# First layer's cross attention: another order of TensorE's work inside a step

## The chip, the cores and the metric

The kernel runs on one core of a Trainium2 chip. It is one launch that computes a whole two-layer decoder. The metric is the device time of that launch in microseconds (us), as the median of several runs. TensorE is called PE below, VectorE DVE, ScalarE ACT, GpSimd POOL and SyncE SP.

## The reference, cut to what matters

The first layer does self attention, cross attention, and a mixture of experts; the second layer follows. Only the cross attention matters here:

```
x = _layernorm(x + _L0_attn_ref(...))
x = _layernorm(x + _L0_xattn_ref(x, ctx_2048, ctx_2048, L0_xattn_gamma))   # this one
...
# inside _L0_xattn_ref: q, k, v are [32, 64, 256]; 8 heads cut the 64 rows in eights,
# the attention runs over the 256 columns
qk = jnp.einsum('bhdq,bhdl->bhql', qh, kh) * scale
sm = jax.nn.softmax(qk, axis=-1)
ret = jnp.einsum('bhql,bhdl->bhdq', sm, vh)
```

So there are 32 x 8 = 256 heads, each with a 256 x 256 matrix of scores over a depth of only 8.

## The kernel before, in words

The 2048 rows of x are 16 tiles of 128 rows; a tile holds two batch entries, so 16 heads. `cross_attention` works in **steps**; a step is two heads, and eight steps (`STEPS`) are a tile. Tile s owns steps 8s to 8s+7, and n is the step's number in its tile. Three things happen to a head, in different steps:

- **First pass** (`first_pass`, PE, L964). The scores of two heads with 3 x 8 x 3 = 72 rows of contraction (q and k are split into bf16 parts), four matmuls of 256 columns into one of two PSUM buffers `a_s` and `a_pt` (even and odd steps). DVE reduces the whole buffer to the negated maxima of 512 rows (`maxima`, L866, output `b_nm`). The first pass of a step waits for the maxima of the step two earlier, since they share a buffer.
- **Second pass** (`second_pass`, PE, L995), 14 steps later (`LAG`). The same scores with three more rows that hold the maxima, two matmuls for each head, into `a_qkv` (even head) or `a_y` (odd head). ACT takes the exponentials (`exps`, L918) into `a_late`. The second pass of a head waits for the exponentials of the head two earlier.
- **Values** (`values`, PE, L1010), from 17 steps on. Four heads are multiplied by their values in one call, into `a_o`: for each of two halves of the keys (`lh`), four matmuls with 32 output columns each, side by side in the array. They are f32, and each matmul is two instructions, so a call shows as sixteen. It runs in every second step. When two calls have filled both halves of `a_o`, ACT copies them out (`products_out`, L924), and the next call waits for that copy.

Small work hangs on single steps. After the last step of a tile DVE splits the maxima in three bf16 parts (`split_maxima`, L879 to L887); PE turns them at n = 2 (`turn_maxima`, L982), ACT copies them (`maxima_out`, L930), SP sends them into the operands of the second pass. At n = 4 DVE takes reciprocals of the denominators of the tile three back (`inverse`, L891), at n = 6 the statistics of its norm (L897, L899). At n = 4 PE turns the normed tile of four back (`turn`, L1020) and ACT copies it (L934).

Each engine runs its own instructions in the order in which they are written, and semaphores link them. The order inside a step on PE was:

```
first_pass(step) ; turn_maxima ; second_pass(both heads) ; values(four heads, every second step) ; turn
```

The first six first passes (`AHEAD`) stand in the self attention before. Steps 6 to 13 have a first pass alone, 14 to 127 have first and second pass, 128 to 141 a second pass alone. When all 16 tiles are normed, the mixture of experts starts.

Of the kernel before, what the change touches and what calls it, by code (L numbers as in the profile page):

```python
# [25 lines left out]
P = 128  # L26
B, T, D = 32, 64, 256
NTOK = B * T
TILES = NTOK // P
SEQS = P // T  # L30
KD = D // P
# [30 lines left out]
class Kernel:  # L62
# [23 lines left out]
    def sem(self, name):  # L86
        self.sems.append(self.nc.alloc_semaphore(name=name))
        return self.sems[-1]
# [579 lines left out]
def cross_attention(k, ctx, free):  # L668
# [3 lines left out]

    nc, io, sem = k.nc, k.io, k.sem
    G, DT, L = P // 8, 8, D
    ROWS = 9 * DT
    SCALE = float(DT) ** -0.5
    STEPS = G // 2
    LAG = STEPS + 6  # L680
    HEADS_2 = G // 2
    qparts = nc.dram_tensor("qparts", (TILES, 3, DT, G, L), BF16, kind="Internal").ap()
    def sb(name, shape, dt=F32):
        return k.sb("b_" + name, shape, dt, ctx)

    def many(count, name, shape, dt=F32):
        return [sb(f"{name}{v}", shape, dt) for v in range(count)]
# [4 lines left out]
    ks, qs = ([space.take([G, L], BF16) for space in (front, middle)] + [sb(n, [P, G, L], BF16)] for n in ("ks", "qs"))  # L692
    vt = many(2, "vt", [P, KD, G, 32])
    nm, nrest, mp = many(2, "nm", [P, 2 * G]), many(2, "nrest", [P, 2 * G]), many(2, "mp", [P, 3, 2 * G], BF16)
    mt = many(2, "mt", [96, P], BF16)
    pr, os_, nd = late.many(8, [KD, L]), end.many(2, [4, L]), end.many(3, [4, L])
# [3 lines left out]
    s2 = [bank[:].rearrange("p (a n) -> p a n", n=L) for bank in (qkv_bank, y_bank)]  # L700
    o_ps = o_bank[:].rearrange("p (a b) n -> p a (b n)", a=2)
# [3 lines left out]
    split, vt_done = sem("b_split"), sem("b_vt_done")  # L705
# [5 lines left out]
    s2_full, s2_out, pv_done, o_out = sem("b_s2_full"), sem("b_s2_out"), sem("b_pv_done"), sem("b_o_out")  # L711
# [7 lines left out]
    T_AT, REC_AT, STATS_AT, TURN_AT = 2, 4, 6, 4  # L719
# [6 lines left out]
    def live(t):  # L726
        return 0 <= t < TILES
# [185 lines left out]
    def scalar(act):  # L913
        def exps(x, g):
            act.wait_ge(s2_full, G * x + g + 1)
            if g % 4 == 0 and 4 * x + g // 4 >= 2:
                act.wait_ge(pv_done, 4 * x + g // 4 - 1)
            act.activation(pr[g % 8][:], s2[g % 2][:], ACT.Exp, scale=SCALE).then_inc(s2_out, 1)  # L918

        def products_out(t, half):  # L920
            act.wait_ge(pv_done, 4 * t + 2 * half + 2)
            if t >= 2:
                act.wait_ge(nd_in[(t - 2) % 3], 64 * ((t - 2) // 3 + 1))
            act.activation(os_[t % 2][:, 2 * half:2 * half + 2, :], o_ps[:], ACT.Copy).then_inc(o_out, 1)  # L924

        def maxima_out(t):
            act.wait_ge(mp_turned, t + 1)
            if t >= 2:
                act.wait_ge(m_placed[t % 2], 16 * (t // 2))
            act.activation(mt[t % 2][:], trb[0:96, :], ACT.Copy).then_inc(mt_out, 1)  # L930

        def turned_out(t):
            act.wait_ge(rn_turned, t + 1)
            act.activation(k.residT[:, :, t * P:(t + 1) * P], tr[:, 0:KD, :], ACT.Copy).then_inc(rT_out, 1)  # L934

        for step in range(LAST):
            s, n = divmod(step, STEPS)
            if n == T_AT and live(s - 1):
                maxima_out(s - 1)
            x, j = divmod(step - LAG, STEPS)  # L940
            if live(x):
                exps(x, 2 * j)
            y, at = divmod(step - LAG - 4, STEPS)
            for half in range(2):
                if at == 4 * half + 2 and live(y):
                    products_out(y, half)
            if live(x):
                exps(x, 2 * j + 1)
            if n == TURN_AT and live(s - 4):
                turned_out(s - 4)  # L950

    def first_pass(pe, step):
        s, n = divmod(step, STEPS)
        if n % 4 == 0:
            pe.wait_ge(placed[s % 3][n // 4], 64 * (s // 3 + 1) + (16 if n == 0 else 0))
        if step == 0:
            pe.wait_ge(free.shifted, TILES)
        elif step == 1:
            pe.wait_ge(free.pt_out, TILES)
        else:  # L960
            pe.wait_ge(s1_out, step - 1)
        for g in (2 * n, 2 * n + 1):
            for qh in range(2):
                ins = pe.matmul(s1[step % 2][:, g % 2, qh, :], qs[s % 3][0:ROWS, g, qh * P:(qh + 1) * P],  # L964
                                ks[s % 3][0:ROWS, g, :], start=True, stop=True)
        ins.then_inc(s1_full, 1)
# [5 lines left out]
    def tensor(pe):  # L972
        def turn_maxima(t):
            if t == 0:
                pe.wait_ge(free.qT_out, TILES)
                pe.wait_ge(free.kbd_out, 4 * TILES)
            pe.wait_ge(m_split, t + 1)
            if live(t - 4):
                pe.wait_ge(rT_out, t - 3)
            if t >= 1:  # L980
                pe.wait_ge(mt_out, t)
            pe.transpose(trb[0:96, :], mp[t % 2][:].rearrange("p a n -> p (a n)"), k.identb[:]).then_inc(mp_turned, 1)  # L982

        def second_pass(x, j):
            if x == 0 and j == 0:
                pe.wait_ge(free.qk_out, TILES)
                pe.wait_ge(free.v_out, 2 * TILES)
                pe.wait_ge(free.y_out, TILES)
            if j == 0:
                pe.wait_ge(m_placed[x % 2], 16 * (x // 2 + 1))  # L990
            for g in (2 * j, 2 * j + 1):
                if G * x + g >= 2:
                    pe.wait_ge(s2_out, G * x + g - 1)
                for lh in range(KD):
                    ins = pe.matmul(s2[g % 2][:, lh, :], ks[x % 3][0:ROWS + 3, g, lh * P:(lh + 1) * P],  # L995
                                    qs[x % 3][0:ROWS + 3, g, :], start=True, stop=True)
                ins.then_inc(s2_full, 1)

        def values(x, q):
            pe.wait_ge(s2_out, G * x + 4 * q + 4)  # L1000
            if x == 0 and q == 0:
                pe.wait_ge(free.o_out, TILES)
            if q == 0:
                pe.wait_ge(vt_done, 2 * x + 2)
            if q % 2 == 0 and 2 * x + q // 2 > 0:
                pe.wait_ge(o_out, 2 * x + q // 2)
            for lh in range(KD):
                for j in range(4):
                    g = 4 * q + j
                    ins = pe.matmul(o_ps[32 * j:32 * j + 32, q % 2, :], vt[x % 2][:, lh, g, :], pr[g % 8][:, lh, :],  # L1010
                                    start=(lh == 0), stop=(lh == KD - 1))
            ins.then_inc(pv_done, 1)

        def turn(t):
            pe.wait_ge(rn_done, t + 1)
            pe.wait_ge(mt_out, min(t + 4, TILES))
            if t >= 1:
                pe.wait_ge(rT_out, t)
            for kd in range(KD):
                ins = pe.transpose(tr[:, kd, :], nd[t % 3][:, 3, kd * P:(kd + 1) * P], k.ident[:])  # L1020
            ins.then_inc(rn_turned, 1)

        for step in range(LAST):
            s, n = divmod(step, STEPS)
            if live(s) and step >= AHEAD:
                first_pass(pe, step)
            if n == T_AT and live(s - 1):
                turn_maxima(s - 1)
            x, j = divmod(step - LAG, STEPS)
            if live(x):  # L1030
                second_pass(x, j)
            y, at = divmod(step - LAG - 3, STEPS)
            if live(y) and at % 2 == 0:
                values(y, at // 2)
            if n == TURN_AT and live(s - 4):
                turn(s - 4)

    return (Programs(sync, gpsimd, scalar, vector, tensor),
            Programs(sync_between, gpsimd_between, None, vector_between, tensor_between))

# [7 lines left out]
def layer0_cross_attention(k):  # L1048
# [3 lines left out]
    with k.memory as ctx:  # L1052
        second, between = cross_attention(k, ctx, free)
        with k.nc.Block() as block:
            @block.sync
            def _(sp):
                first.sync(sp, between.sync)
                second.sync(sp)

            @block.gpsimd  # L1060
            def _(gp):
                first.gpsimd(gp, between.gpsimd)
                second.gpsimd(gp)

            @block.scalar
            def _(act):
                first.scalar(act)
                second.scalar(act)

            @block.vector  # L1070
            def _(dve):
                first.vector(dve, between.vector)
                second.vector(dve)

            @block.tensor
            def _(pe):
                first.tensor(pe, between.tensor)
                second.tensor(pe)
# [2099 lines left out]
```

## Time and profile before

| | before |
|---|---|
| median of 3 runs | 1250.38 us (1249.96 to 1255.8) |
| the profiled execution's own time | 1244.66 us |
| its span | 1242.6 us |
| PE, DVE, ACT, POOL busy | 1103.5, 800.7, 585.0, 454.7 us |
| mean granted PE clock | 0.969 of full |

The span goes from the first to the last instruction of the profiled execution. A busy PE in this table is not a PE at its peak, since the ends of matmuls are modelled and neighbours overlap; what the engine can do is read from the distance between starts. The cross attention fills the span from about 163 us (its first first pass) to about 427 us (its last transpose).

### The profile page before, as it was taken

The page shows a single profiled execution, that of the slowest core. Times are in us where ns is not written, and L with a number is a line of the kernel's source. Part 1 is how long each engine was busy: PE and PEld are TensorE (multiplying, and loading weights), DVE is VectorE, ACT ScalarE, POOL GpSimd, SP SyncE. Part 2 cuts the span into 40 slices and gives each one's busy share as a digit, 9 for nine tenths or more (in the row PEclk, how much of TensorE's full clock was granted, in tenths as well). Part 3 has the DMA queues.
Part 4 walks back from the last instruction along what each step waited for, and adds up shares of the span by engine and source line. Part 5 has one row for each costly group of instructions (what it writes and reads, how often), then busy time and mean ns, then how long its engine had stood idle before and what let it go on. Part 6 is the DMA issues. An engine that isn't in the chain of part 4 may idle for free. (4 is left out here: it accounts for less than half of the span.)

```text
span 1242.6 us, 20732 instructions
## 1 busy us (share of the span) xinstructions
PE 1103.5 (89%) x7356; PEld 652.4 (53%) x7356; DVE 800.7 (64%) x1547; ACT 585.0 (47%) x1209; POOL 454.7 (37%) x692
## 2 busy tenths in 40 slices
PE   6888769998998599999878999869997999999997
PEld 3566535454554245777433555647775343545455
DVE  4899886888886142333576668647885456465555
ACT  2666506766767331343376555348773422121110
POOL 6999851555534245333235346431111000000001
PEclk9999978999999799999999999989997999999999
DMA  6964354655662112453503000020000000000000
GB/s 219 309 192 143 94 131 106 147 139 142 149 143 73 47 56 97 125 170 120 174 1 135 1 1 1 1 69 2 2 2 5 21 1 0 9 9 9 8 9 26
DMA packets 75354, 95.90 MB, mean 77 GB/s; under 512 B 12883, under 2 KB 62189, under 8 KB 74573
## 3 DMA queue, kind: packets, MB, share of 16 engines
q1 hardware_dynamic: 70835, 84.92, 24.1%
q0 software_dynamic: 3408, 9.34, 2.1%
q8 instruction: 61, 1.00, 0.3%
q10 hardware_dynamic: 1010, 0.31, 0.1%
q14 instruction: 40, 0.33, 0.1%
HBM read 57.47 MB, written 31.27 MB: 71 GB/s over the span
## 5 line engine op out<-in xcount | busy, mean ns | idle before, releaser
L918 ACT ACTIVATE a_late<-a_qkv 128x512 f32<-128x512 f32 x128 | 77.3, 604 | 59.3 <-PE a_qkv L995 59.3
L2654 POOL TENSOR_SCALAR f_rstd<-f_mv 128x1 f32<-128x1 f32 x16 | 3.8, 239 | 266.5 <-DVE f_mv L2793 266.4
L866 DVE TENSOR_REDUCE b_nm<-a_s 128x4 f32<-128x1024 f32 x64 | 78.0, 1219 | 30.8 <-PE a_s L964 30.8
L2738 DVE TENSOR_TENSOR f_prod<-f_sg,f_kept 128x512 f32<-128x512 f32 (+1 forms) x48 | 33.2, 692 | 96.4 <-ACT f_kept L2683 93.5
L2863 PE MATMUL fps_h<-residT,w_f_w 128*128 128x512 f32 x176 | 82.4, 608 | 2.5 <-DVE f_inner L2775 2.5
L866 DVE TENSOR_REDUCE b_nm<-a_pt 128x4 f32<-128x1024 f32 x64 | 76.7, 1199 | 2.3 <-PE a_pt L964 2.3
L918 ACT ACTIVATE a_late<-a_y 128x512 f32<-128x512 f32 x128 | 77.0, 602 | 0.0
L2677 ACT ACTIVATE f_sg<-fps_h 128x512 f32<-128x512 f32 (+1 forms) x24 | 14.3, 596 | 125.2 <-PE fps_h L2882 108.3
L1010 PE MATMUL a_o<-a_late,b_vt 128*32 128x256 f32 x1024 | 69.2, 389 | 0.0
L1320 POOL DMA_INDIRECT routed<-c_out,c_target x39 | 37.4, 959 | 67.2 <-ACT c_out L1401 66.9
L1974 DVE SCALAR_TENSOR_TENSOR d_acc<-d_pad,d_cw,d_acc 128x512 f32<-128x512 f32 x72 | 58.4, 815 | 4.9 <-ACT d_acc L1880 3.2
L350 POOL TENSOR_TENSOR a_nrm<-a_ss,phalf 128x20 f32<-128x20 f32 x16 | 56.9, 3559 | 3.5 <-DVE a_ss L472 3.5
L2863 PEld LDWEIGHTS fps_h<-residT,w_f_w 128*128 128x128 f32 x176 | 33.3, 193 | 42.1 <-issue 37.7
L1520 DVE TENSOR_TENSOR c_hid<-c_sg,cps_h 128x176 f32<-128x176 f32 x39 | 13.2, 338 | 63.1 <-ACT c_sg L1395 63.1
L1582 PE MATMUL cps_h<-c_wgu,c_xT 128*128 x156 | 52.7, 461 | 0.6 <-ACT c_xT L1389 0.6
L2100 PE MATMUL cps_h<-residT,d_win 128*128 128x512 f32 x96 | 46.6, 617 | 3.4 <-ACT d_zs L1873 1.9
L838 POOL TENSOR_TENSOR a_rest<-a_rest 128x256 f32<-128x256 f32 x16 | 11.6, 723 | 96.1 <-DVE a_rest L891 96.1
L1805 POOL TENSOR_TENSOR d_rs<-d_ms,mhalf 128x4 f32<-128x4 f32 x16 | 22.4, 1400 | 65.7 <-DVE d_ms L2031 65.7
L1314 POOL DMA_INDIRECT xrows<-c_xr,c_place_int x32 | 31.0, 967 | 35.0 <-DVE c_xr L1490 19.8
L2677 ACT ACTIVATE f_sg<-f_kept 128x512 f32<-128x512 f32 (+1 forms) x24 | 15.1, 630 | 60.1 <-DVE f_kept L2743 60.1
L1010 PEld LDWEIGHTS a_o<-a_late,b_vt 128*32 128x32 f32 x1024 | 26.9, 110 | 25.1 <-issue 14.0
L1601 PE MATMUL cps_o<-c_wd,c_hT 88*128 x156 | 40.1, 380 | 0.0
(428 smaller groups left out, 2896.9 us busy)
## 6 DMA issues: line engine op xcount, KB each, us to landing
kparts<-a_rest SPq DMA_DIRECT2D x48, 192.0 KB, 3.8
a_rest<-a_rest SPq DMA_DIRECT2D x64, 128.0 KB, 3.0
xrows<-in_c_fill SPq DMA_DIRECT2D x13, 387.0 KB, 4.5
c_xrow<-xrows SPq DMA_DIRECT2D x39, 129.0 KB, 2.1
c_back<-routed SPq DMA_DIRECT2D x16, 256.0 KB, 3.6
a_front<-kparts SPq DMA_DIRECT2D x12, 288.0 KB
a_front<-qparts SPq DMA_DIRECT2D x36, 96.0 KB
qparts<-b_xp SPq DMA_DIRECT2D x48, 64.0 KB, 2.8
```

Source lines behind the costliest of these rows:

```text
L350: gp.tensor_tensor(nrm[v][:], ss[v][:], k.phalf[:, 0:H20], ALU.pow).then_inc(rooted, 1)
L866: dve.tensor_reduce(nm[s % 2][:, 4 * n:4 * n + 4].rearrange("p (g h) -> p g h", h=2), s1[step % 2][:], AX.X, ALU.max, negate=True).then_in ...
L918: act.activation(pr[g % 8][:], s2[g % 2][:], ACT.Exp, scale=SCALE).then_inc(s2_out, 1)
L1010: ins = pe.matmul(o_ps[32 * j:32 * j + 32, q % 2, :], vt[x % 2][:, lh, g, :], pr[g % 8][:, lh, :], start=(lh == 0), stop=(lh == KD - 1))
L1314: gp.indirect_dma_start(k.xrows[:], bass.IndirectOffsetOnAxis(ap=place_int[n][:, t:t + 1], axis=0), xr[:, t, :], None).then_inc(scattered[ ...
L1320: gp.indirect_dma_start(routed[:], bass.IndirectOffsetOnAxis(ap=target[s % 8][:], axis=0), out[s % 4][:], None).then_inc(sent[s % 4], 16)
L1582: ins = pe.matmul(h_ps[s % 2][:, 0:2 * F], xT[s % 2][:, kd, :], wgu[:, kd, ds(e, 1), :].rearrange("p a f -> p (a f)"), start=(kd == 0), st ...
L1601: ins = pe.matmul(o_ps[:, s % 2, 0:D], hT[s % 2][:, c, :], wd2[:, ds(e, 1), c, :].rearrange("p a f -> p (a f)"), start=(c == 0), stop=(c = ...
L1974: ins = dve.scalar_tensor_tensor(out=acc[v][:], in0=pad[v][:, :, tap:tap + T], scalar=cw[:, m, tap:tap + 1], in1=acc[v][:], op0=ALU.mult, ...
L2100: ins = pe.matmul(bank[:], win[:, kd, m * P:(m + 1) * P] if m < XT else wz[:, kd, (m - XT) * P:(m - XT + 1) * P], k.residT[:, kd, c * CHUN ...
L2738: dve.tensor_tensor(prod[n % 2][at], sg[n % 2][at], up, ALU.mult).then_inc(prod_done, 1)
L2863: pe.matmul(h_ps[j][:], (w1, w3)[j][:, kd, m * P:(m + 1) * P], k.residT[:, kd, c * CHUNK:(c + 1) * CHUNK], start=(kd == 0), stop=False)
```

## The change

The PE step is written in another order, and the calls are cut smaller. `second_pass` now takes one head, `values` one half of the keys of four heads. A step is now: half a `values` call, the second pass of the even head, the first pass, `turn_maxima`, the second pass of the odd head, `turn`. ACT's step follows it: `products_out` first, then the even head's exponentials, `maxima_out`, the odd head's exponentials. A blank line moves the numbers of the lines behind it by one.

```
@@ scalar (ACT) @@
-            if n == T_AT and live(s - 1):
-                maxima_out(s - 1)
-            x, j = divmod(step - LAG, STEPS)
-            if live(x):
-                exps(x, 2 * j)
             y, at = divmod(step - LAG - 4, STEPS)
             for half in range(2):
                 if at == 4 * half + 2 and live(y):
                     products_out(y, half)
+            x, j = divmod(step - LAG, STEPS)
+            if live(x):
+                exps(x, 2 * j)
+            if n == T_AT and live(s - 1):
+                maxima_out(s - 1)
             if live(x):
                 exps(x, 2 * j + 1)
@@ tensor (PE) @@
+        def values(x, q, lh):
+            if lh == 0:
+                pe.wait_ge(s2_out, G * x + 4 * q + 4)
+                if x == 0 and q == 0:
+                    pe.wait_ge(free.o_out, TILES)
+                if q == 0:
+                    pe.wait_ge(vt_done, 2 * x + 2)
+                if q % 2 == 0 and 2 * x + q // 2 > 0:
+                    pe.wait_ge(o_out, 2 * x + q // 2)
+            for j in range(4):
+                g = 4 * q + j
+                ins = pe.matmul(o_ps[32 * j:32 * j + 32, q % 2, :], vt[x % 2][:, lh, g, :], pr[g % 8][:, lh, :],
+                                start=(lh == 0), stop=(lh == KD - 1))
+            if lh == KD - 1:
+                ins.then_inc(pv_done, 1)
...
         for step in range(LAST):
             s, n = divmod(step, STEPS)
+            y, at = divmod(step - LAG - 3, STEPS)
+            if live(y):
+                values(y, at // KD, at % KD)
+            x, j = divmod(step - LAG, STEPS)
+            if live(x):
+                second_pass(x, 2 * j)
             if live(s) and step >= AHEAD:
                 first_pass(pe, step)
             if n == T_AT and live(s - 1):
                 turn_maxima(s - 1)
-            x, j = divmod(step - LAG, STEPS)
             if live(x):
-                second_pass(x, j)
-            y, at = divmod(step - LAG - 3, STEPS)
-            if live(y) and at % 2 == 0:
-                values(y, at // 2)
+                second_pass(x, 2 * j + 1)
             if n == TURN_AT and live(s - 4):
                 turn(s - 4)
```

**Two steps on PE where everything runs** (steps 22 and 23; `b_ks,b_qs` are the operands of the first pass, `a_middle` those of the second). Before:

```order
L964 MATMUL a_s<-b_ks,b_qs 128x256 x4
L995 MATMUL a_qkv<-a_middle 128x256 x2
L995 MATMUL a_y<-a_middle 128x256 x2
L964 MATMUL a_pt<-b_ks,b_qs 128x256 x4
L995 MATMUL a_qkv<-a_middle 128x256 x2
L995 MATMUL a_y<-a_middle 128x256 x2
L1010 MATMUL a_o<-a_late,b_vt 32x256 x8
```

Now, from the half call that opens step 22:

```order
L1010 MATMUL a_o<-a_late,b_vt 32x256 x4
L995 MATMUL a_qkv<-a_middle 128x256 x2
L965 MATMUL a_s<-b_ks,b_qs 128x256 x4
L995 MATMUL a_y<-a_middle 128x256 x2
L1010 MATMUL a_o<-a_late,b_vt 32x256 x4
L995 MATMUL a_qkv<-a_middle 128x256 x2
L965 MATMUL a_pt<-b_ks,b_qs 128x256 x4
L995 MATMUL a_y<-a_middle 128x256 x2
```

The count of matmuls is the same. The block of eight that stood between two odd-to-even pairs is now two blocks of four, one ahead of each even head, and the first pass stands between the two heads.

**Where the second pass sets in, on PE** (steps 14 and 15). Before:

```order
L964 MATMUL a_s<-a_middle 128x256 x4
L995 MATMUL a_qkv<-a_front 128x256 x2
L995 MATMUL a_y<-a_front 128x256 x2
L964 MATMUL a_pt<-a_middle 128x256 x4
L995 MATMUL a_qkv<-a_front 128x256 x2
L995 MATMUL a_y<-a_front 128x256 x2
```

Now:

```order
L995 MATMUL a_qkv<-a_front 128x256 x2
L965 MATMUL a_s<-a_middle 128x256 x4
L995 MATMUL a_y<-a_front 128x256 x2
L995 MATMUL a_qkv<-a_front 128x256 x2
L965 MATMUL a_pt<-a_middle 128x256 x4
L995 MATMUL a_y<-a_front 128x256 x2
```

The first pass of step 14 now stands behind the first head of the second pass, and so behind that head's wait for the maxima that a DMA brings.

**A step with products_out on ACT** (step 20 and its neighbours). Before:

```order
L918 ACTIVATE a_late<-a_y 128x512
L918 ACTIVATE a_late<-a_qkv 128x512
L924 ACTIVATE a_rest<-a_o 128x512
L918 ACTIVATE a_late<-a_y 128x512
L918 ACTIVATE a_late<-a_qkv 128x512
```

Now:

```order
L919 ACTIVATE a_late<-a_y 128x512
L925 ACTIVATE a_rest<-a_o 128x512
L919 ACTIVATE a_late<-a_qkv 128x512
L919 ACTIVATE a_late<-a_y 128x512
```

The copy of the products has moved from between the two heads to ahead of both.

## Rows read from the trace of the kernel before

**Rows 1.** Windows: us, then busy (instructions) of each engine, granted clock, DMA share, GB/s.

```profile
172.00:196.00 24.00, 18.63 (x89) 10.01 (x90) 18.23 (x25) 4.89 (x10) 11.12 (x21) 0.50 0.48 112
203.00:392.00 189.00, 170.04 (x1721) 94.08 (x1723) 162.35 (x210) 132.27 (x263) 85.33 (x139) 1.00 0.56 137
392.00:416.00 24.00, 18.39 (x201) 7.81 (x193) 6.60 (x12) 18.02 (x37) 8.61 (x14) 1.00 0.22 57
```

**Rows 2.** Waits, 203 to 392 us: who waited for whom, us in total, times, longest.

```profile
ACT a_late L918 <- PE a_qkv L995: 44.6, 40, 1.2
PEld a_y L995 <- ACT a_late L918: 32.4, 53, 0.9
DVE b_nm L866 <- PE a_s L964: 25.4, 27, 1.5
```

**Rows 3.** PE timeline (start, us, what): the first passes opening tiles 3 and 15.

```profile
205.72 0.61 PE L964 MATMUL a_s<-a_front 72*128 72x256 bf16 x4
...
378.20 0.61 PE L964 MATMUL a_s<-a_front 72*128 72x256 bf16 x4
```

**Rows 4.** PE timeline, parts of three steps near 300 us.

```profile
300.06 0.39 PE L1020 MATMUL a_tr<-ident,a_rest 128*128 128x128 f32 x2
300.28 0.60 PE L964 MATMUL a_pt<-a_front 72*128 72x256 bf16 x4
...
301.67 0.39 PE L995 MATMUL a_y<-a_middle 75*128 75x256 bf16 x2 [0.57 <-ACT a_late L918]
301.99 1.07 PE L1010 MATMUL a_o<-a_late,b_vt 128*32 128x256 f32 x16
303.00 0.61 PE L964 MATMUL a_s<-a_front 72*128 72x256 bf16 x4
303.44 0.38 PE L995 MATMUL a_qkv<-b_qs,b_ks 75*128 75x256 bf16 x2
303.67 0.38 PE L995 MATMUL a_y<-b_qs,b_ks 75*128 75x256 bf16 x2
303.88 0.60 PE L964 MATMUL a_pt<-a_front 72*128 72x256 bf16 x4
304.52 0.39 PE L995 MATMUL a_qkv<-b_qs,b_ks 75*128 75x256 bf16 x2
```

**Rows 5.** PE timeline inside that values call: its second and its last group.

```profile
302.23 0.83 PE L1010 MATMUL a_o<-a_late,b_vt 128*32 128x256 f32 x12
...
302.67 0.40 PE L1010 MATMUL a_o<-a_late,b_vt 128*32 128x256 f32 x4
```

**Rows 6.** DVE timeline, the same tile from n = 4 on.

```profile
300.96 1.74 DVE L891 RECIPROCAL a_rest<-a_rest 128x256 f32<-128x256 f32 x1
302.62 1.16 DVE L866 TENSOR_REDUCE b_nm<-a_pt 128x4 f32<-128x1024 f32 x1
303.70 1.21 DVE L866 TENSOR_REDUCE b_nm<-a_s 128x4 f32<-128x1024 f32 x1
304.82 0.42 DVE L897 BATCH_NORM_STATS2 b_stats<-a_rest 128x6 f32<-128x256 f32 x1
...
305.38 1.19 DVE L866 TENSOR_REDUCE b_nm<-a_pt 128x4 f32<-128x1024 f32 x1
...
307.69 1.22 DVE L866 TENSOR_REDUCE b_nm<-a_s 128x4 f32<-128x1024 f32 x1
```

**Rows 7.** ACT timeline, two exponentials behind one another.

```profile
303.86 0.60 ACT L918 ACTIVATE a_late<-a_qkv 128x512 f32<-128x512 f32 x1 [0.99 <-PE a_qkv L995]
304.36 0.59 ACT L918 ACTIVATE a_late<-a_y 128x512 f32<-128x512 f32 x1
```

**Rows 8.** PE timeline, the first head of the second pass.

```profile
186.56 0.58 PE L995 MATMUL a_qkv<-a_front 75*128 75x256 bf16 x2 [1.63 <-DMA a_front<-b_mt]
```

**Rows 9.** PE timeline, the values calls of steps 127 and 141 with 143.

```profile
391.57 1.07 PE L1010 MATMUL a_o<-a_late,b_vt 128*32 128x256 f32 x16
...
413.88 2.00 PE L1010 MATMUL a_o<-a_late,b_vt 128*32 128x256 f32 x32
```

More of the change, by code:

```diff
@@ L982, in turn_maxima, with second_pass @@
             pe.transpose(trb[0:96, :], mp[t % 2][:].rearrange("p a n -> p (a n)"), k.identb[:]).then_inc(mp_turned, 1)
-        def second_pass(x, j):
-            if x == 0 and j == 0:
+        def second_pass(x, g):
+            if x == 0 and g == 0:
                 pe.wait_ge(free.qk_out, TILES)
@@ L988, in second_pass @@
                 pe.wait_ge(free.y_out, TILES)
-            if j == 0:
+            if g == 0:
                 pe.wait_ge(m_placed[x % 2], 16 * (x // 2 + 1))
[L991 to L1006, printed above, removed]
-            for lh in range(KD):
[L1008 to L1012, printed above, removed]
+            if G * x + g >= 2:
+                pe.wait_ge(s2_out, G * x + g - 1)
+            for lh in range(KD):
+                ins = pe.matmul(s2[g % 2][:, lh, :], ks[x % 3][0:ROWS + 3, g, lh * P:(lh + 1) * P],
+                                qs[x % 3][0:ROWS + 3, g, :], start=True, stop=True)
+            ins.then_inc(s2_full, 1)
+        def values(x, q, lh):
[13 more added lines that the diff above has]
+                ins.then_inc(pv_done, 1)
         def turn(t):
```

## The prediction

> **What bounds the kernel now.** I looked first at the windows over the cross attention, because the change touches nothing else [rows 1]. From 203 to 392 us, where first and second pass run together, no engine is full: DVE works 162 of 189 us and ACT 132. PE shows 170, but its ends are modelled, so I take nothing from that and read starts instead. The waits say how the engines hold each other up [rows 2]: ACT stood 44.6 us for the even head's scores from PE, PE's weight loads stood 32.4 us for ACT's exponentials, and DVE stood 25.4 us for the first pass. A ring of two engines that wait for each other in turn is the sign that an order sets the pace, not a throughput. The pace itself: tiles 3 and 15 open 172.48 us apart [rows 3], so a tile takes 14.37 us and a step 1.80.
>
> The PE timeline shows the ring [rows 4]. Free of waits, a first pass takes 0.44 us (303.00 to 303.44), the even head 0.23, the odd head 0.21, together 0.88 a step. The values call costs 301.67 to 303.00 less the odd head's 0.21, so 1.12. Two steps would be 2 x 0.88 + 1.12 = 2.88 us, a tile four times that and 0.28 for transposes (0.22 for the pair at 300.06 to 300.28; 0.06 is my estimate for the single bf16 one, as a quarter of that pair), 11.8 us. The tile takes 14.37, so 2.6 us of it are PE standing. Why it stands: behind the odd head come the values call and the next first pass, 1.56 us in which ACT gets nothing, while it has work for one or two exponentials, 0.50 us apart [rows 7]. It idles 0.99 us, and then PE must wait for it, because only two score buffers exist: 304.52 instead of 304.32, and 0.57 us of wait at 301.67.
>
> **The change, part by part.** No instruction of arithmetic is added or dropped, and no DMA is moved in SP's or POOL's queue. Four costs and gains are left.
>
> *The gap before the even head.* It falls from 1.56 us in every second step to one half of a values call in each step; the first pass (0.44) now stands in the other gap. With the half call at 0.68 (next item) neither gap exceeds what ACT's buffer covers. Checked on one step of PE, from zero: half call to 0.68, even head, first pass at 0.91, odd head at 1.35, next step at 1.56. The even head's scores are full at 0.68 + 0.38 (the length of its row) + 0.04 (303.82 to 303.86 [rows 4, 7]) = 1.10; its exponentials end at 1.70, and their buffer is wanted at 1.56 + 0.68 = 2.24. The odd head: full at 1.77, done 2.37, wanted 2.91. So PE waits for ACT no more, with 0.5 us to spare, and also holds in a step with products_out (about 0.5 more on ACT): that copy starts once the half call is done, near 0.75, ends at 1.35, and the next values half wants it at 1.56. This slack of 0.2 is the thinnest of the design.
>
> *The split of the values call.* A call of four groups starts at 301.99, the second group at 302.23, the last at 302.67, the next first pass at 303.00 [rows 4, 5]. Entry costs 0.11 (301.67 + 0.21 to 301.99), first to second group 0.24, last group to the next work 0.33. A half call is two groups: 0.11 + 0.24 + 0.33 = 0.68. Two are 1.36 against 1.12, so the split costs 0.24 for two steps, about 1 us a tile. No row shows a call of two groups. Lower bound: the split is free (0.56 a half, PE step 1.44). Upper bound: a half costs as much as a whole, 1.12. I take 0.68, since entry and exit are read on the very same kinds of neighbours.
>
> The Trainium skill speaks against this part: TensorEngine Tiling (Array Packing), Key Properties, says that changing the tiling mode drains TensorE, and the values use a quarter of the columns each while the scores use all. Its page TensorE: Matmul & The Clock Gate, Single matmul latency, puts a drain near 175 ns. As an estimate from those pages, 0.175 at each end of a half in place of the 0.11 and 0.12 of the rows would make the half 0.80. The trace agrees that there is a cost at each end, of 0.11 and (0.33 less 0.21) 0.12.
>
> *PE's and DVE's need in a tile.* PE: 8 x (0.88 + 0.68) + 0.28 = 12.8 us. DVE: 14.37 less its wait for the first pass, 25.4 us over 189/14.37 = 13.2 tiles, 1.93 [rows 2]: 12.4 us. Both lie near each other, so one must walk through a tile. Values [rows 4, 6]: buffer full 0.64 after the first pass starts; maxima follow each other every 1.12 (303.70 to 304.82), and release the buffer 1.22 + 0.05 after they start; reciprocal 1.66, statistics 0.56, split of the maxima 305.38 to 307.69 less 1.12, 1.19. Start the clock when DVE begins the maxima of n = 0 with the buffer of n = 1 full. First pass 2 waits for that buffer: 1.27. Then PE sets the pace: 2.89, 4.45. Maxima: 0, 1.12, 2.24, 3.53, 5.09 (idle 0.6 in all). The reciprocal then holds DVE until 7.87, while PE puts first passes at 6.23 and 7.79; maxima 5 at 7.87, 6 at 8.99, statistics, 7 at 10.67, and the next tile's 0 at 12.98. PE's first passes 9.35, 10.91, 12.47 find free buffers; the next waits until 14.25, which is 1.27 in the new tile. So the walk closes: **13.0 us a tile**, PE standing 0.2, DVE 0.6. The gain is 1.4 us a tile.
>
> *Start and end.* Step 14's first pass now waits with the second pass for the maxima's DMA at 186.56 [rows 8], where PE had done it earlier. It costs one first pass at the half clock, which the window shows as 0.50 [rows 1], so 2 x 0.44 = about 0.9 us, a little less as PE was standing before. From 391.57 on the second pass is alone, 22.3 us for 14 steps, 1.59 a step [rows 9]. There PE needs 0.68 + 0.44 = 1.12, but the two heads stand together again; ACT's second exponential ends 0.50 + 0.60 behind the first's start, so every other step loses 0.24, and products_out adds 0.6 in four steps: about 1.35. Gain 14 x 0.24 = 3.4 us. What comes behind (DMA of the quotients, last norm, experts) depends on the last tile alone and moves as a block.
>
> **Sum.** At full clock 109 of the 114 common steps lie in the stretch, 13.6 tiles: 13.6 x 1.37 = 18.7. With 3.4 for the end and -0.9 for the start: 21 us. The profiled execution took 1244.66 us, so it would take about 1223.5. It is itself 5.7 below the median of 1250.38, so against that median I forecast 1229.5.
>
> **The rivals.**
>
> A. *Both ends of a half call cost more* (0.80 a half by the pages' drain, worked out above as an estimate). As a mechanism of this kernel: each entry and exit lies bare. PE's tile is 8 x 1.68 + 0.28 = 13.7; gain 0.65 x 13.6 = 8.8, end 2, start -0.9: 10 us, 1240. For it: four switches for two steps. Against: both ends are in the rows, smaller. 0.10.
>
> B. *The split is free, DVE becomes the bound.* Then a tile is DVE's 12.4: 1.93 x 13.6 + 3.4 - 0.9 = 29 us, 1221. For it: neighbouring work might fill entry and exit. Against: nothing did in the 1.12. 0.11.
>
> C. *A wait takes the wait's place; no change.* The odd head now stands behind the first pass, and that behind DVE. DVE spends 3.4 us a tile outside the maxima; if PE stands for 1.4 of it or more, with ACT dry behind, nothing is won and the time stays near 1250. The same follows if the copy of the products, with its slack of 0.2 us, is late by 0.7 in each of its two places a tile. My walk has PE standing 0.2. 0.09.
>
> D. *Slower: a half costs nearly a whole.* If the 16 weight loads of a call are what hides the latency inside it, and two groups can't, a half may reach 1.12 and PE's tile 8 x 2.00 + 0.28 = 16.3: +1.9 x 13.6 = 26 us, less what the end gives, 1274. It decides from a half of (14.37 - 0.28)/8 - 0.88 = 0.88 us on. Against: groups follow each other every 0.22 inside the call, so the two of a half have no reason to take more. 0.06.
>
> **How the numbers follow.** My case has 0.64, with 1224 to 1238 for its own range (a half of 0.63 to 0.74 moves PE's tile by 0.4 either way, 6 us). A measurement here tells about 0.5%, 6 us, from no change. Faster by more: my case, A and B, 0.85. Within: C, 0.09. Slower: D, 0.06. The range 1218 to 1243 holds my case, A and B, and leaves out C and D.
>
> **What the new profile would show.** The starts of tiles 3 and 15 about 156 us apart instead of 172.5. The wait of ACT for the even head's scores falls from 44.6 us to under 10 in the same stretch, PE's waits for ACT to near none, and DVE's wait for the first pass to about 8 of 25. A half call: two groups 0.24 apart, and 0.33 to the even head. From step 128 on, 1.35 us a step. I am wrong if PE's loads wait for DVE's maxima by more than 1 us a tile, if the first group of a values call waits for products_out, or if a half call takes over 0.8.

## The result, and the profile after

| | before | changed |
|---|---|---|
| median | 1250.6 us (4 runs) | 1371.51 us (4 runs, 1371.16 to 1381.35) |
| profiled execution, its span | 1244.66, 1242.6 | 1381.35, 1379.3 |
| mean granted PE clock | 0.969 | 0.836 |

The changed kernel is slower: the ratio is 1.097, interval 1.092 to 1.102. The forecast was 1229.5 us with a range of 1218 to 1243. It was wrong by its sign and by 142 us. The profiled execution of the changed kernel is the longest of its runs: the medians differ by 120.9 us, the two profiled executions by 136.7.

The windows of the changed kernel, with the columns of [rows 1]; the second to fourth cover the cross attention from shortly before tile 3 opens:

```profile
172.00:196.00 24.00, 18.59 (x86) 9.03 (x87) 19.34 (x26) 4.83 (x9) 12.55 (x25) 0.51 0.39 94
203.00:392.00 189.00, 189.00 (x1073) 85.13 (x1070) 109.67 (x128) 90.36 (x162) 53.95 (x88) 0.50 0.33 89
392.00:513.00 121.00, 121.00 (x687) 54.86 (x679) 68.98 (x85) 57.51 (x104) 33.05 (x54) 0.50 0.30 78
513.00:552.00 39.00, 30.46 (x200) 10.61 (x199) 9.06 (x15) 19.42 (x38) 10.76 (x15) 0.59 0.16 45
```

Read the first engine's column and the one behind the engines together. PE is busy for 189.00 of 189.00 us, so it never stands, and the granted clock is 0.50, the lower of its two levels (1.2 GHz), for all of it. Before, the same window had 1.00 [rows 1]. Both kernels are at about 0.5 from 172 to 196 us. Before rose there; the changed one did not. The rise of before lies behind its first values call, as its PE timeline shows:

```profile
192.62 1.94 PE L1010 MATMUL a_o<-a_late,b_vt 128*32 128x256 f32 x16
194.49 1.03 PE L964 MATMUL a_s<-b_ks,b_qs 72*128 72x256 bf16 x4
...
196.13 0.60 PE L964 MATMUL a_pt<-b_ks,b_qs 72*128 72x256 bf16 x4
```

The first pass at 194.49 has the length of the lower level, the next one, at 196.13, that of full clock.

One step and the openings of tiles 3 and 15 in its PE timeline (to be held against [rows 3, 4]):

```profile
211.91 1.08 PE L1010 MATMUL a_o<-a_late,b_vt 128*32 128x256 f32 x8
212.92 0.61 PE L995 MATMUL a_qkv<-a_middle 75*128 75x256 bf16 x2
213.32 1.06 PE L965 MATMUL a_s<-a_front 72*128 72x256 bf16 x4
214.18 0.64 PE L995 MATMUL a_y<-a_middle 75*128 75x256 bf16 x2
214.74 1.08 PE L1010 MATMUL a_o<-a_late,b_vt 128*32 128x256 f32 x8
...
491.30 1.06 PE L965 MATMUL a_s<-a_front 72*128 72x256 bf16 x4
```

A first pass takes 0.86 us (213.32 to 214.18), not 0.44, a step 2.83 (211.91 to 214.74), not the 1.56 of the forecast. Tiles 3 and 15 open 277.98 us apart, against 172.48 before: 23.2 us a tile. Where the 136.7 us between the two spans lie: 7.6 before tile 3 opens, 105.5 from tile 3 to tile 15, 14.5 from there to the experts' first matmul (429.10 before, 556.70 now), and 9.1 behind it, in code that the change does not touch; the other runs of the changed kernel are some 10 us shorter as a whole, so I take that last part for one of this single execution.

Its waits from 203 to 392 us:

```profile
ACT a_late L919 <- PE a_qkv L995: 47.9, 49, 1.1
PEld a_qkv L995 <- ACT a_late L919: 46.2, 57, 0.8
ACT a_late L919 <- PE a_y L995: 40.8, 66, 0.7
DVE b_nm L867 <- PE a_s L965: 40.7, 26, 1.6
DVE b_nm L867 <- PE a_pt L965: 38.6, 32, 1.7
```

Before, ACT and PE took turns in waiting [rows 2]. Now ACT and DVE both wait for PE, for both heads and both buffers. The weight loads (PEld) still wait for ACT, 46.2 us, but they run ahead of the matmuls, and the matmuls show no stand in this window. So PE, at half its speed, is the bound.

### The profile page after: what moved, and what is told of

Same layout as the page of the kernel before. It is cut to its first block and busy times, and to the rows that moved or that the text cites. A ratio compares the mean times of both kernels' runs of the same rounds, so it can differ in the third digit from the quotient of the medians.

```text
span 1379.3 us, 20732 instructions
## 1 busy us (share of the span) xinstructions
PE 1269.0 (92%) x7356; PEld 707.9 (51%) x7356; DVE 814.1 (59%) x1547; ACT 599.7 (43%) x1209; POOL 455.7 (33%) x692
## 5 line engine op out<-in xcount | busy, mean ns | idle before, releaser
L1010 PE MATMUL a_o<-a_late,b_vt 128*32 128x256 f32 x1024 | 137.0, 629 | 0.4 <-ACT a_late L919 0.4
L2103 PE MATMUL cps_h<-residT,d_win 128*128 128x512 f32 x96 | 51.3, 671 | 2.7 <-ACT residT L1366 1.4
L892 DVE RECIPROCAL a_rest<-a_rest 128x256 f32<-128x256 f32 x16 | 27.9, 1743 | 24.6 <-DMA a_rest<-a_rest 24.6
```

Of the source, the lines that this page charges most:

```text
L2103: ins = pe.matmul(bank[:], win[:, kd, m * P:(m + 1) * P] if m < XT else wz[:, kd, (m - XT) * P:(m - XT + 1) * P], k.residT[:, kd, c * CHUN ...
```

## The experiments

The theory H after the result: a values call cut in halves never lets the clock rise from the lower level, whatever else stands around it. (The last clause turns out too strong, as the end of the third experiment shows.) Its rivals: the denser order itself holds the clock down (D), or the new order at the start misses the moment of the rise (S).

**Whole values calls in the new order.**

```
-            if live(y):
-                values(y, at // KD, at % KD)
+            if live(y) and at % 2 == 0:
+                values(y, at // 2, 0)
+                values(y, at // 2, 1)
```

> The changed kernel, with the values calls whole again (both halves of the keys behind one another, in every second step, at the step's start); the order of the rest stays changed. Theory H (cutting the values call in halves keeps the granted clock at the half through the cross attention): the clock rises near 196 us as it did before, the stage has 1.00, and the time is 1225 to 1240. Rival D (the denser order itself, with PE never standing, holds the clock down): the clock stays at 0.50 and the time near 1360. Rival S (the new order at the start, steps 14 to 18, misses the moment at which the clock rises, and it gets no second one): also near 1360.

Measured: 1236.31 us beside 1254.55 for before, ratio 0.988 (0.983 to 0.993). Its windows:

```profile
172.00:196.00 24.00, 18.11 (x103) 9.66 (x102) 17.77 (x24) 5.96 (x12) 10.16 (x20) 0.54 0.42 99
203.00:350.00 147.00, 140.72 (x1469) 83.63 (x1466) 137.89 (x181) 115.70 (x224) 77.73 (x128) 1.00 0.62 157
```

The clock rose near 194 us and held through this window. DVE is busy 138 of 147 us, 94%, and tiles take 12.97 us. D and S both fall: density and start are those of the changed kernel. The split alone makes the difference of 135 us.

**Halves in the old order.** PE's order is again first pass, both heads, values; the half call stands at the end of every step. On ACT `maxima_out` goes back ahead of both exponentials, and `products_out` stays at the head of the step. Of PE's edit the new lines are shown:

```
+            if live(x):
+                second_pass(x, 2 * j)
+                second_pass(x, 2 * j + 1)
+            y, at = divmod(step - LAG - 2, STEPS)
+            if live(y):
+                values(y, at // KD, at % KD)
```

> The order of before on PE (first pass, both heads of the second pass, then values), but the values call in halves, one at the end of each step from the 16th on, and products_out at the head of ACT's step. H: the clock stays at 0.50 through the stage and the time is 1350 or more. Rivals D and S: the clock rises near 196 us as before, since order and density are those of before; the time is 1240 to 1255.

Measured: 1380.96 us, ratio 1.103 (1.098 to 1.109). Tiles take 23.3 us. Its window from 203 to 392 us:

```profile
203.00:392.00 189.00, 189.00 (x1069) 85.32 (x1066) 108.74 (x127) 84.96 (x161) 54.27 (x88) 0.50 0.35 88
```

The same picture as in the changed kernel, with the order of before. So the order is not needed for the loss, and the halves are enough for it.

**Whole calls in the first two tiles only.** The condition of the first experiment's edit becomes `y < 2`, halves otherwise.

> The changed kernel, with whole values calls for the first two tiles and halves for the other 14. It tells apart rising from falling. H in its weak form (halves only prevent the rise): the clock rises in the first two tiles and stays at 1.00, a tile then takes about 13.0 us as forecast, and the time is 1225 to 1240. H in its strong form (halves also pull it down): it rises and falls again within a few tiles, 1330 or more. Rival D: it never rises or falls at once, near 1370.

Measured: four runs of 1248.87, 1265.27, 1258.93 and 1234.99 us, beside 1254.55 for before. Only one lies in the range expected of the weak form, none in that of the strong form. The mean granted clock of the four goes the same way: 0.943, 0.930, 0.939 and 0.959. The trace, of the first of them, says why. Steps at full clock, and then one late transfer:

```profile
352.84 0.64 PE L1010 MATMUL a_o<-a_late,b_vt 128*32 128x256 f32 x8
353.41 0.39 PE L995 MATMUL a_qkv<-a_front 75*128 75x256 bf16 x2
353.64 0.60 PE L965 MATMUL a_pt<-b_ks,b_qs 72*128 72x256 bf16 x4
354.08 0.38 PE L995 MATMUL a_y<-a_front 75*128 75x256 bf16 x2
354.39 0.64 PE L1010 MATMUL a_o<-a_late,b_vt 128*32 128x256 f32 x8
...
362.96 0.39 PE L995 MATMUL a_qkv<-a_middle 75*128 75x256 bf16 x2 [1.44 <-DMA a_middle<-b_mt]
363.19 0.60 PE L965 MATMUL a_s<-b_ks,b_qs 72*128 72x256 bf16 x4
363.63 0.38 PE L995 MATMUL a_y<-a_middle 75*128 75x256 bf16 x2
363.94 1.06 PE L1010 MATMUL a_o<-a_late,b_vt 128*32 128x256 f32 x8
```

and its windows before and behind that place:

```profile
203.00:350.00 147.00, 143.11 (x1466) 79.98 (x1463) 137.29 (x176) 119.56 (x223) 76.09 (x124) 1.00 0.62 158
363.00:398.00 35.00, 35.00 (x207) 15.11 (x207) 18.69 (x26) 17.78 (x33) 9.45 (x14) 0.51 0.17 44
```

Once the clock is up, halves hold it: they run from the opening of tile 4, near 220 us, so for 130 us at 1.00, a step of 1.55 us (352.84 to 354.39), most tiles 12.9 to 13.1 us. Then PE stood 1.44 us for the maxima's DMA, the clock fell, and the halves left it down for the next 35 us, with PE again 35.00 of 35.00 busy. The weak form of H holds up to that fall, and a wait is found that the forecast did not have. The kernel with whole calls in all tiles had such a wait too, of 1.70 us, ended at 359.38, and its windows around it are the contrast:

```profile
356.00:361.00 5.00, 3.30 (x44) 1.97 (x37) 4.03 (x4) 3.07 (x6) 1.45 (x2) 1.00 0.66 162
361.00:368.00 7.00, 7.00 (x47) 3.60 (x39) 4.45 (x10) 3.24 (x7) 3.34 (x5) 0.51 0.35 79
368.00:373.00 5.00, 4.97 (x51) 3.12 (x53) 4.00 (x4) 3.95 (x9) 0.00 (x0) 1.00 0.02 5
```

There the clock fell just so, and was back after 7 us, behind the next whole call that ran at the lower level (365.08).

The halves had a way back too, though a late one. In all four profiles in which half calls reached the end stretch at the lower level (this one, the changed kernel, the halves in the old order, and the short calls below) the clock rose there, where no first pass stands beside the second any more. The changed kernel, 29 us behind its last first pass:

```profile
539.22 0.63 PE L1021 MATMUL a_tr<-ident,a_rest 128*128 128x128 f32 x2
539.78 1.08 PE L1010 MATMUL a_o<-a_late,b_vt 128*32 128x256 f32 x8
540.79 0.43 PE L995 MATMUL a_qkv<-a_front 75*128 75x256 bf16 x2
541.07 0.38 PE L995 MATMUL a_y<-a_front 75*128 75x256 bf16 x2
541.38 0.64 PE L1010 MATMUL a_o<-a_late,b_vt 128*32 128x256 f32 x8
```

In each of the four the rise came directly behind an f32 transpose and a half call side by side. The same pair had stood once a tile before, from tile 4 on, and in the changed kernel once more in the end stretch (522.95 us), without a rise. So H holds for the stretch in which first and second pass run together, which is where the loss is, and not for whatever else stands around a half call.

**Halves in four tiles, whole calls behind.** The condition becomes `y >= 4`.

> The changed kernel with halves for the first four tiles and whole values calls for the other twelve. H: the clock stays at 0.50 until the values of tile 4 begin (about 290 us) and rises there; four tiles at 22.7 us and the rest at 13 to 13.5 give 1262 to 1275. Rival S: once missed it stays down, near 1360. Rival D: the same, near 1360.

Measured: 1278.73 us, ratio 1.020 (1.014 to 1.025), 4 above the expected range. Tiles of 22.8 to 23.2 us, then of 12.96 to 13.3, the last ones of 14.0 to 16.5 with the waits for the maxima's DMA that the third experiment showed. The PE timeline where the first whole call stands:

```profile
279.67 1.08 PE L1010 MATMUL a_o<-a_late,b_vt 128*32 128x256 f32 x8
280.69 0.61 PE L995 MATMUL a_qkv<-a_middle 75*128 75x256 bf16 x2
281.09 1.06 PE L965 MATMUL a_s<-a_front 72*128 72x256 bf16 x4
281.94 0.63 PE L995 MATMUL a_y<-a_middle 75*128 75x256 bf16 x2
282.51 1.94 PE L1010 MATMUL a_o<-a_late,b_vt 128*32 128x256 f32 x16
284.38 0.61 PE L995 MATMUL a_qkv<-a_middle 75*128 75x256 bf16 x2
284.78 0.90 PE L965 MATMUL a_pt<-a_front 72*128 72x256 bf16 x4
285.52 0.39 PE L995 MATMUL a_y<-a_middle 75*128 75x256 bf16 x2
```

Some 90 us of halves at the lower clock (the values begin near 192 us), then the first whole call at 282.51, and 0.74 us (284.78 to 285.52) for a first pass that would take 0.86: the clock rose right behind it. There was no chance missed at the start; S is dead a second time. The same holds through all nine profiles of kernels with whole calls (before, before with the queue of the last experiments, and seven others): the clock rose 1.8 to 3.6 us after the start of the first whole call, here 2.9.

**What in the whole call does it?** First, the scores almost alone: the half calls of the first four tiles multiply 8 of 256 columns, so that part of the values is left out.

```
+            cols = 8 if x < 4 else L
             for j in range(4):
                 g = 4 * q + j
-                ins = pe.matmul(o_ps[32 * j:32 * j + 32, q % 2, :], vt[x % 2][:, lh, g, :], pr[g % 8][:, lh, :],
+                ins = pe.matmul(o_ps[32 * j:32 * j + 32, q % 2, 0:cols], vt[x % 2][:, lh, g, :], pr[g % 8][:, lh, 0:cols],
```

> The changed kernel, whose half calls of the first four tiles multiply 8 of the 256 query columns only, so that part of the values is left out there; the other twelve tiles have full half calls. It asks what in the whole values call raised the clock. Theory G (the bare entry and exit of every half call, 0.28 us of PE in 2.8 at the half clock, keep it from rising): these gaps stay, and a larger share of the step is gaps, so the clock stays at 0.50 and a tile takes about 15 us in the first four and 23.2 behind. Theory W (what counts is how much of a stretch is the four-wide f32 work of the values, and the first passes and second passes weigh less): it stays at 0.50 too. Rival R (the score matmuls raise it, and the half calls only dilute them): the clock rises in the first four tiles; then, as the halves at full clock hold it, the others run at about 13.0 us a tile and the time is below 1245.

Measured in a single execution: 1340.56 us. Its window over the tiles with short calls:

```profile
203.00:254.00 51.00, 51.00 (x403) 31.34 (x400) 39.28 (x49) 32.34 (x60) 17.92 (x30) 0.50 0.48 121
```

The short call costs 0.23 us, PE is full, and the clock stays at 0.50; tiles take 16.5 to 16.9 us, not the 15 expected: a step is 2.05 us (209.85 to 211.90), of which 1.82 are the scores at that clock. Rival R falls: bf16 score matmuls nearly behind one another do not raise the clock here.

Then as many entries and exits as in the changed kernel, but the four-wide work bunched: the call of one step takes 248 query columns for both halves of the keys, that of the next the last 8. The lines that differ are shown in part:

```
+            a, b = (0, L - 8) if lh == 0 else (L - 8, L)
+            for h in range(KD):
...
+                    ins = pe.matmul(o_ps[32 * j:32 * j + 32, q % 2, a:b], vt[x % 2][:, h, g, :], pr[g % 8][:, h, a:b],
+                                    start=(h == 0), stop=(h == KD - 1))
```

> The changed kernel with a values call in every step as there, but cut by query columns instead of by keys: one call multiplies 248 of the 256 columns for both halves of the keys (as long a run as a whole call), the next the last 8. So there are as many entries and exits of the four-wide mode as with halves, and the run of every second step has its full length. Theory G (the entries and exits hold the clock down): 0.50 through the stage, 1360 or more. Theory W (the length of unbroken four-wide work is what counts): the clock rises near 195 us and the time is 1236 to 1245. The two could not be told apart by the earlier runs.

Measured: 1238.59 us, ratio 0.988 (0.984 to 0.991). Two calls of it while the clock was still low, and its window:

```profile
206.10 0.40 PE L1012 MATMUL a_o<-a_late,b_vt 128*32 128x8 f32 x16
206.44 0.61 PE L995 MATMUL a_qkv<-a_middle 75*128 75x256 bf16 x2
206.84 1.06 PE L965 MATMUL a_s<-b_ks,b_qs 72*128 72x256 bf16 x4
207.69 0.64 PE L995 MATMUL a_y<-a_middle 75*128 75x256 bf16 x2
208.25 1.88 PE L1012 MATMUL a_o<-a_late,b_vt 128*32 128x248 f32 x16
```

```profile
203.00:350.00 147.00, 145.12 (x2111) 92.87 (x2104) 133.08 (x172) 112.03 (x214) 74.19 (x122) 0.97 0.60 151
```

The clock rose near 211 us, 14 to 18 us later than in the kernels with whole calls: three long calls of 1.8 us (190.79, 196.68, 202.47) went by without it, and it came behind the fourth. The columns multiplied in two steps, the entries and the exits are those of the changed kernel; their distribution differs, and there are twice as many matmuls and weight loads for them (32 instructions in two steps, not 16). So the entries and exits (theory G) are not what kept the clock down. That the bunching of the four-wide work (theory W) raised it is the reading that fits all runs; that the doubled count of instructions helped here was not tested by itself, but whole calls raise the clock without it.

**The late transfer.** SP's queue is reordered: a tile's maxima go ahead of the store of the tile four back and the load of the next keys.

```
+            if live(s - 1):
+                maxima_rows(s - 1)
             if live(s - 4):
                 store(s - 4)
             if live(s + 1):
                 load(sp, s + 1, 0)
-            if live(s - 1):
-                maxima_rows(s - 1)
```

With whole calls in all tiles:

> The kernel with whole values calls and the changed order, and SP's queue issues the maxima of a tile ahead of the store of the tile four back and the load of the next tile's keys, not behind them. Theory: the last three tiles of that kernel took 13.7, 13.8 and 15.6 us instead of 13.0 because the maxima's DMA stands behind five others and lands 4.9 us after its issue, late by 0.9 to 1.7 us. Ahead of them it lands in time: 13.0 us for all tiles, some 3 to 4 us off the 1236. Rival: the transfers themselves are slow there and the place in the queue does not matter, 1236; or the loads pushed back become late, slower.

Whole calls in all tiles and the queue as it was, measured beside it:

> The kernel with whole values calls and the changed order once more, unchanged, as the measure on this chip for the two others: 1236 against a before of 1250 to 1255.

Whole calls in the first two tiles, halves behind, and the new queue:

> The kernel with whole calls in the first two tiles and halves in the rest, with the same change of SP's queue. There the first wait of 1.4 us for the maxima's DMA, near 361 us, was followed by a fall of the clock that lasted 37 us, and the four runs lay between 1235 and 1265. Theory: without that wait the clock holds, a tile stays at 13.0, and the runs draw together at 1230 to 1236. Rival: the halves lose the clock at any small pause, and the runs stay spread over tens of us.

Measured: whole calls with that queue 1230.77 us, ratio 0.986 (0.982 to 0.991), beside 1241.39 for whole calls without it (0.993, 0.990 to 0.996). With it the waits for the maxima are gone and most tiles take 12.97. Tile 15 opens 13.9 us behind tile 14, since a wait of 0.77 us for the queries' load has come up, and here too the clock fell, for 3.4 us:

```profile
359.25 0.61 PE L965 MATMUL a_s<-a_front 72*128 72x256 bf16 x4 [0.77 <-DMA a_front<-qparts]
...
360.01 1.92 PE L1010 MATMUL a_o<-a_late,b_vt 128*32 128x256 f32 x16
```

The profile of whole calls without the new queue is that of the fastest of its ten runs, 1233.02 us. It shows some 4 us of late tiles and no fall in this stretch, so it does not account for all of the 10.6 us between the two medians, where 3 to 4 were expected. Two whole tiles, halves behind, and that queue: 1229.31 us, ratio 0.984 (0.979 to 0.989), four runs from 1225 to 1230. Its windows:

```profile
203.00:370.00 167.00, 164.66 (x1685) 91.27 (x1681) 157.77 (x205) 137.90 (x257) 84.00 (x136) 1.00 0.66 154
373.00:395.00 22.00, 19.48 (x198) 6.75 (x197) 7.55 (x15) 18.71 (x38) 9.59 (x15) 1.00 0.20 62
```

And before with the new queue:

> The kernel before, with the maxima's DMA ahead of the store and the load in SP's queue and nothing else. Before, nothing waits for that DMA between 203 and 392 us, so the theory expects no change, 1250 within 0.3%; the gain of the kernels with both edits would then be that of TensorE's order, freed of its late transfer. Rival: the queue's order is worth 5 us by itself.

Measured: 1253.99 us beside 1251.66, ratio 1.001 (0.999 to 1.003). The kernel before has no use for the queue's order, as expected; the wait exists at the faster pace only.

The version with two whole tiles once more:

> The fastest version once more: whole values calls for two tiles, halves behind, maxima first in SP's queue. 1225 to 1232 in all runs if the clock is safe once it is up and no transfer is late; single runs over 1240 if it still falls now and then.

Measured: 1229.62 us, ratio 0.982 (0.980 to 0.985). Five of six runs lie from 1227 to 1232, one at 1251.77. So the sign that the expectation named came up once: the mean granted clock of that run is 0.940, of the other five 0.953 to 0.964. Where it fell is not known, since that run had no profile. The third experiment showed no way back up for halves before the end stretch, and whole calls in all tiles with the same queue had no run over 1235.15, in four. Of these two, equal in their medians, I would take whole calls in all tiles.

## Why the prediction was wrong, step by step

- **The step that failed** is the sum's first line, "At full clock 109 of the 114 common steps lie in the stretch", and *Start and end* ahead of it, which priced the half clock as one first pass, 0.9 us. Both took the rise near 196 us as given, so a tile was to take 13.0 us and took 23.2 at a granted clock of 0.50, which over twelve tiles makes a loss of 105.5 us where the sum has a gain. The rise was a product of the very call that the change cuts. Shown by the first, second and fourth experiment: whole calls raise the clock in the new order, halves do not in the old one, and the rise comes with the first whole call wherever that stands.
- **The gap before the even head.** Right. At full clock the order makes 12.96 us a tile where the walk gave 12.98. But the split has no part in it: whole calls in the new order give 12.97. The waits were mis-sized: ACT still stood for the even head's scores 22.8 us of 167 in the version with two whole tiles, not under 10, while DVE's wait for the first pass on `a_s` fell to 4.1, less than the 8 expected. PE's weight loads stood 12.4 us for ACT in the same window, where near none was forecast; it cost the tile nothing, as its 12.96 us say.
- **The split's direct cost.** Right, 1.55 us a step against 1.56. Rivals A and D, both about a half call's length at full clock, had no part in the loss. A half call costs 0.67: 0.57 (352.84 to 353.41) and an entry of 0.10, against 0.68 forecast. The Trainium skill, TensorEngine Tiling (Array Packing), Key Properties, says that a change of tiling mode drains TensorE; with the prediction's estimate of that drain a half would have been 0.80, and this trace does not bear out a price of that size.
- **The end.** Right in size: 373.04 to 391.35 for 14 steps, 1.31 a step against 1.35.
- **The slack of products_out.** Seldom short: in the version with two whole tiles the values calls waited for that copy three times between 203 and 370 us, 0.6 us together, and twice in the end stretch, 0.3 us at most.
- **The slow side.** Rival D forecast 1274 by a lengthened half call. The true mechanism was not among the rivals; the half clock stood in [rows 1] and was costed only as a start.
- **A wait not forecast**, the maxima's DMA behind five others in SP's queue, costs 5 to 11 us once a tile takes 13 us (1241.39 against 1230.77 on one chip; 1236.31 was measured on another).
- With the clock up and that transfer in time, the two versions measured 1229.3 and 1230.8 us, beside the forecast of 1229.5. Neither is the kernel of the forecast: both have whole calls where the clock must rise, and a queue that the change leaves alone. The agreement says that the walk through a tile was sound, not that the prediction was.

## What to carry to other kernels

Where a profile shows the granted clock low at the entrance of a long stretch, ask what raises it, and whether the change touches that work; the price is the whole stretch at half speed, not the ramp. A busy PE does not prove that its clock will rise: this one was full from 203 to 513 us and stayed at 0.50. A long unbroken call can be worth keeping for the clock alone, and once an order is faster, look through the DMA queue for the transfer that comes late next.

## What the runs showed of the hardware that was not expected

- PE at a busy share of 1.00 was granted 0.50 through 310 us of the two middle windows. The Trainium skill, TensorE: Matmul & The Clock Gate, Part 1, says that the default state is throttled and activity releases the throttle. This trace does not bear that out for activity as the profile's busy share has it.
- The two levels are sticky in this mix of work. Halves held 1.00 for 130 us in one kernel (for 175 us, 220 to 395, with the new queue), and 0.50 for 310 us in another, with the same instructions in the same order.
- At 0.50, bf16 scores almost alone (51 us), and scores with a four-wide f32 call of 1.0 us in every step, did not raise the clock. The same f32 work in a call of 1.9 us in every second step did, each time within 4 us of the start of the first such call; cut to 248 columns, only behind the fourth. At the end, without first passes, an f32 transpose beside a half call was enough, though not each time. What the chip counts in it stays open.
- Short stands of PE were followed by a fall of the clock about 1 us after their end: of 1.44 and 1.70 us for the maxima, of 0.77 for the queries. But stands of 1.26 and 1.25 us, in the second run of whole calls (333.91 and 348.11), were not, so the length of the stand alone does not say which.
